# Attention keys on TensorE: 162 contracted rows as two runs of 81, or as 128 for all images and 64 on one half of the array for each pair

## The reference, cut to what matters

```python
q_flat = x.reshape(bs, 1, c * hw)
k_flat = k1.reshape(bs, 1, c * hw)
kq = jnp.stack([q_flat, k_flat], axis=2).reshape(bs, 2 * hw, c)
a = jax.nn.relu(_bn(jnp.einsum('oi,bic->boc', se_att_w1, kq), se_att_bn))
```

## Time and profile before

| | us |
|---|---|
| median of 3 runs | 1763.16 (1757.49 to 1765.74) |
| profiled execution, its time | 1758.98 |
| profiled execution, its span | 1757.3 |
| PE busy | 1375.9 |
| DVE busy | 1140.7 |
| ACT busy | 802.5 |
| POOL busy | 649.3 |

### The profile page before, as it was taken

How to read it: one execution, slowest core, us unless ns; L and a number is a source line. 1 busy time by engine, 2 the same in 40 slices (tenths; PEclk the granted TensorE clock), 3 DMA queues, 4 the chain that set the end, 5 groups by cost and what they waited for, 6 DMA issues and landing times.

```text
span 1757.3 us, 38235 instructions
## 1 busy us (share of the span) xinstructions
PE 1375.9 (78%) x9764; PEld 1122.8 (64%) x9765; DVE 1140.7 (65%) x3074; ACT 802.5 (46%) x1779; POOL 649.3 (37%) x561
## 2 busy tenths in 40 slices
PE   0297888889999999999755555499999999999300
PEld 0286888856666666666555555388888888888300
DVE  7795333328676767676488888566666666666493
ACT  0393444434443444443399998233333333333250
POOL 0161111113333333333066667245454545445200
PEclk9997787879999999999555555699999999999755
DMA  8535453566767675764133433423332323232475
GB/s 305 129 90 194 182 190 142 196 191 162 178 147 181 145 181 147 177 149 111 50 111 123 127 125 124 137 88 87 88 93 87 87 87 96 86 94 73 188 312 242
DMA packets 259238, 250.50 MB, mean 143 GB/s; under 512 B 150105, under 2 KB 234414, under 8 KB 255172
## 3 DMA queue, kind: packets, MB, share of 16 engines
q1 hardware_dynamic: 238895, 196.95, 38.5%
q0 software_dynamic: 20320, 53.28, 9.2%
HBM read 152.07 MB, written 105.57 MB: 147 GB/s over the span
## 4 chain that ended last, share of the span: by engine, by line
PE 68%; DVE 11%; ACT 7%; DMA 6%; issue 3%; SPq 3%; DVEq 0%; ACTq 0%; POOLq 0%; POOL 0%
PE ps L690 14%; PE ps L675 13%; PE ps L514 6%; PE ps L497 5%; PE ps L463 4%; PE ps L541 3%; PE ps L569 3%; PE ps L565 2%; DMA u_d<-in_zstrings 2%; ACT pool_ L1255 2%; PE ps L524 2%; PE ps L659 2%; DVE big L1211 2%; PE ps L533 2%; PE ps L567 2%
## 5 line engine op out<-in xcount | busy, mean ns | idle before, releaser
L1482 POOL DMA_INDIRECT y_d<-pool_,to_s x176 | 254.7, 1447 | 282.8 <-DVE pool_ L1171 248.2
L690 PE MATMUL ps<-pool_,aux 128*128 x2112 | 248.1, 273 | 5.1 <-DVE aux L1163 3.2
L675 PE MATMUL ps<-aux,pool_ 128*128 128x256 f16 x2112 | 246.2, 273 | 0.8 <-ACT aux L1383 0.6
L690 PEld LDWEIGHTS ps<-pool_,aux 128*128 128x128 f16 x2112 | 197.5, 98 | 50.0 <-issue 23.7
L675 PEld LDWEIGHTS ps<-aux,pool_ 128*128 x2112 | 206.3, 98 | 25.4 <-issue 1.5
L1383 ACT ACTIVATE aux<-ps,b_s 128x256 f32<-128x256 f32 x352 | 138.0, 474 | 161.9 <-DVE aux L1163 161.6
L1462 POOL DMA_INDIRECT rows_d<-aux,idx_s x162 | 160.0, 988 | 109.6 <-DVE idx_s L1074 60.2
L1171 DVE SCALAR_TENSOR_TENSOR pool_<-ps,pool_ 128x512 f32<-128x512 f32 x88 | 60.9, 692 | 138.9 <-PE ps L690 138.9
L1454 POOL DMA_DIRECT2D pool_<-v_d x64 | 50.0, 781 | 272.5 <-PE ps L571 271.1
L1375 ACT ACTIVATE aux<-ps 128x512 f16<-128x512 f32 x88 | 52.5, 597 | 173.7 <-PE ps L659 173.7
L514 PE MATMUL ps<-pool_,se_w_s 81*81 81x512 f32 x256 | 118.7, 607 | 5.4 <-DMA pool_<-k_d 5.4
(11 more groups left out here) (202 smaller groups left out, 3104.7 us busy)
## 6 DMA issues: line engine op xcount, KB each, us to landing
pool_<-rows_d SPq DMA_DIRECT2D x88, 258.0 KB
pool_<-y_d SPq DMA_DIRECT2D x18, 1152.0 KB, 8.6
big<-in_x SPq DMA_DIRECT2D x2, 5184.0 KB, 21.5
xn_d<-big SPq DMA_DIRECT2D x16, 648.0 KB, 3.0
v_d<-aux SPq DMA_DIRECT2D x64, 162.0 KB, 2.0
ks_d<-aux SPq DMA_DIRECT2D x64, 162.0 KB, 1.9
pool_<-xn_d SPq DMA_DIRECT2D x32, 324.0 KB
pool_<-k_d SPq DMA_DIRECT2D x32, 324.0 KB
```

Source lines behind the costliest of these rows:

```text
L675: last = nc.tensor.matmul(o, w_s[:, a, bass.ds(e * (4 * PIECE) + (k * HID + j * 128), 128)], xh_s[:, par, b, k * SLOTS:(k + 1) * SLOTS], s ...
L690: last = nc.tensor.matmul(ps[:, 6 + par, s * C:(s + 1) * C], hh_s[:, par, a, j, s * 128:(s + 1) * 128], w_s[:, b, bass.ds(e * (4 * PIECE) ...
L1482: nc.gpsimd.indirect_dma_start(out=y_d[:, :], out_offset=bass.IndirectOffsetOnAxis(ap=to_s[:, par, k:k + 1], axis=0), in_=yo_s[:, par, k, ...
```

## The change

Before, each pair of images takes two matmuls of 81 contracted rows (x, then k1), each with 512 moving columns. After, a first matmul contracts 128 rows (x rows 1 to 80 and k1 rows 0 to 47) for both pairs, and a second one 64 rows (x row 0, fifteen rows whose weights are zero, and k1 rows 33 to 80, of which the first fifteen have zero weights): for the pair n = 0 on partitions 0 to 63, for n = 1 on partitions 64 to 127. The number of matmuls stays at four a group, each 512 columns wide. The order changes: both 128-row matmuls, then both 64-row ones, and `se1_p` of n = 0 comes after the third instead of the second. The builder of instructions takes the part of the array from the operands' start partition and size: rows 0 to 63 or 64 to 127 for the last two.

The loads for `keys` become six a group in place of two, and move 128 x 4 + 2 x 64 x 2 = 768 rows of 1 KB in place of 648. Tiles behind `kq_s` move down by 4 KB in each partition. The weights are 128 x 2 x 81 with zeros where a row counts elsewhere.

```diff
-        se_w1_s = sb("se_w1_s", [HW, 2, HW])
+        se_w1_s = sb("se_w1_s", [128, 2, HW])
...
-        kq_s = take(HW, 2, 2, G, C)
+        kqa_s = take(128, 2, G, C)
+        kqb_s = take(128, 2, G // 2, C)
...
                     if not first:
                         sp.wait_ge(S["se1_p"], 2 * g - 2)
-                    for k, src in enumerate((xn_d, k1_d)):
-                        sp.dma_start(kq_s[:, par, k],
-                                     src[rows, :].rearrange("b (i j) -> i b j", j=C)).then_inc(S[f"kq_in{par}"], 16)
+                    xq, kq = (d[rows, :].rearrange("b (i j) -> i b j", j=C) for d in (xn_d, k1_d))
+                    for dst, src in ((kqa_s[0:80, par], xq[1:HW]), (kqa_s[80:128, par], kq[0:48])):
+                        sp.dma_start(dst, src).then_inc(S[f"kq_in{par}"], 16)
+                    for n in range(2):
+                        two = slice(2 * n, 2 * n + 2)
+                        for dst, src in ((kqb_s[64 * n:64 * n + 16, par], xq[0:16, two]),
+                                         (kqb_s[64 * n + 16:64 * n + 64, par], kq[HW - 48:HW, two])):
+                            sp.dma_start(dst, src).then_inc(S[f"kq_in{par}"], 16)
...
-                pe.wait_ge(S[f"kq_in{par}"], 32 * (i + 1))
+                pe.wait_ge(S[f"kq_in{par}"], 96 * (i + 1))
                 if not first:
                     pe.wait_ge(S["a_c"], 2 * g)
                 for n in range(2):
-                    for k in range(2):
-                        last = nc.tensor.matmul(ps[0:HW, n, :], se_w1_s[:, k, :],
-                                                kq_s[:, par, k, 2 * n:2 * n + 2, :].rearrange("p b j -> p (b j)"),
-                                                start=k == 0, stop=k == 1)
-                    last.then_inc(S["se1_p"], 1)
+                    nc.tensor.matmul(ps[0:HW, n, :], se_w1_s[:, 0, :],
+                                     kqa_s[:, par, 2 * n:2 * n + 2, :].rearrange("p b j -> p (b j)"),
+                                     start=True, stop=False)
+                for n in range(2):
+                    half = slice(64 * n, 64 * n + 64)
+                    nc.tensor.matmul(ps[0:HW, n, :], se_w1_s[half, 1, :],
+                                     kqb_s[half, par, :, :].rearrange("p b j -> p (b j)"),
+                                     start=False, stop=True).then_inc(S["se1_p"], 1)
...
+    wx, wk = i["conv_se_att_w1"].T.reshape(2, HW, HW)
+    se_w1 = np.zeros((128, 2, HW), f)
+    se_w1[0:80, 0], se_w1[80:128, 0] = wx[1:], wk[0:48]
+    for n in (0, 64):
+        se_w1[n, 1], se_w1[n + 31:n + 64, 1] = wx[0], wk[48:]
```

More of the change, by code:

```diff
@@ L1563 @@
         "key_bias": np.broadcast_to(i["conv_se_key_b"], (128, HW)),
-        "se_w1": i["conv_se_att_w1"].T.reshape(2, HW, HW).transpose(1, 0, 2), "se_bn": i["conv_se_att_bn"].T,
+        "se_w1": se_w1, "se_bn": i["conv_se_att_bn"].T,
         "se_w2": se_w2, "sa_w1": sa_w1, "sa_bn": halves(i["conv_sa_att_bn"].T), "sa_w2": sa_w2,
```

## The result

| | before | changed |
|---|---|---|
| median, us | 1763.64 (1757.49 to 1765.74, 4 runs) | 1745.18 (1739.83 to 1746.1, 4 runs) |
| profiled execution, its time | 1758.98 | 1739.83 |
| profiled execution, its span | 1757.3 | 1738.1 |

The ratio is 0.9895, with a 95% interval of 0.9873 to 0.9917: 18.5 us faster, clear of the 0.5% that the prediction named as the measurement's limit.

A forecast was written before the change was run, and what follows sets the result against it. PE was taken to bound the attention stage: 28 groups at 0.10 us plus 0.2 for the first gave 3.0, plus 0.7 at the start, 3.7 us saved. On the median's scale that meant 1759.5 us, range 1749 to 1773.

The forecast's parts named there:

- What bounds the stage: Attention stage, 440 to 813 us: PE is always busy at full clock, so PE time saved there is saved.
- the 0.91 us of slack ahead of `band`: DVE's last mask ends 0.91 us before `band` starts, so even 0.54 us saved in `keys` fits.
- The 128-row matmuls for free: In `keys`, columns streamed set the cost, so contracting 128 rows for 81 costs nothing; 0.43 us a record.
- The step that failed: 64-row matmuls in `keys`: records start in program order, so one of four half-array records is hidden, 0.43 us a group.
- rival 2: Cheap changes of shape (1750 us) or full overlap of all four half-array records in `keys` (1747 us); chance 0.20.
- The price of two changes: `keys` switches PE to half rows and back each group, costing 0.27 to 0.375 us.
- the reading by the gap: From gaps in `band`, plus weight loads no longer hidden: two changes of shape cost 0.375 us a group.
- the one by a sum over `band`: Eight `band` records take 1.25 us against 0.71 expected: 0.135 us for each of four changes, 0.27 for two.
- The rule cited against the change: For `keys`' changes to half rows: a change of tiling mode drains TensorE; the rule gives no drain's price.
- Loads: no cost: Six load issues for two take 1.6 us more, within 4.8 us of queue slack and 7 us of landing slack.
- A full spread over sixteen engines: Loads of 80, 48 and 16 partitions using all sixteen DMA engines would transfer in 2.3 us in place of 3.2.
- The stage's start: PE's wait for the first `keys` load shortens by 0.7 us, bounds -1.6 to +1.6.

The follow-up runs named there:

- same-half run: The changed kernel with both 64-row matmuls on the same half of the array (partitions 0 to 63), loads unchanged: 1772.52 us, ratio to before 1.0054.
- two-by-two run: The changed kernel with a further zero-weight 64-row matmul behind each 64-row matmul, on the same half: 1771.47 us, one execution.
- all-rows run: The changed kernel with the second matmuls contracting all 128 rows, zero weights on the other pair's half, loads unchanged: 1758.66 us, ratio to before 0.9977.

## Why the prediction was wrong

- **What bounds the stage: right.** What `keys` saved shows undiminished in the distance of groups, and the 0.91 us of slack ahead of `band` sufficed.
- **The 128-row matmuls for free: right.** Their four records hold PE 1.81 us, of which 0.09 is the change behind them.
- **The step that failed** is "If PE starts them in order, the second of n0 must wait for the first (same rows), the first of n1 may run beside the second of n0, and the second of n1 comes last: three times 0.43 in place of four. I take this, 0.43 us a group". It booked one record of overlap, and the overlap is two, 0.853 us a group (same-half run). The two-by-two run shows why: the halves do not keep a common order. That "every stretch of PE's timeline that I read shows records starting in program order" was no evidence. Overtaking can only be seen where two neighbours use different parts of the array, and the kernel before has no such neighbours in the loop: a matmul on all columns stands between any two narrow ones. The overlapping case stood in the prediction as part of rival 2 with its sum, 0.86 less the price of the changes, 1747 us; it was given too little of a chance, and the range ended above it.
- **The price of two changes** was given as 0.27 to 0.375, and 0.354 was measured. For rows the reading by the gap (0.375) came near, and the one by a sum over `band` (0.27) was too low. The sum was not wrong for columns: the reordered `band` gives 0.13 a change there too. What failed in it is that a price measured on columns was carried over to rows. The sum used the middle, 0.32 or 0.33, which is close to 0.354.
- **The rule cited against the change**, from the Trainium skill, TensorEngine Tiling (Array Packing), Key Properties (a change of mode drains, tiles operate independently), fits both numbers: 0.167 us for each of four changes, and independent halves. The Trainium skill, TensorE: Matmul & The Clock Gate, Part 3, has matmuls start and end in program order. For matmuls on different halves of the rows the two-by-two run contradicts it (eight records in 1.72 + 0.17 us), and the measurement decides. So does it for what the prediction drew from that page, an overlap of one record of four: it is two.
- **Loads: no cost, right, for a partly wrong reason.** The queue's six issues take 2.9 us and not 2.4 (starts 0.51 apart), and there is still time left. A full spread over sixteen engines was expected to bring a faster landing. The shares rose, as forecast, to 1.14 and 1.16 (rows below). The rate was 237 and then 169 GB/s, first above and then below the 205 of the earlier trace rows, and earlier loads may still be among the 237. From the first issue to the end of the transfers it took about as long as before: from 606.34 to about 611.7, and from 616.09 to about 621.4.
- **The stage's start** was given 0.7 us. From the first `keys` to the fifth it took 47.1 us for 48.4 before. The wait for the first load hardly changed: 4.86 us (row below) for 5.08. In the profiled executions of the seven kernels with six loads the first `keys` began at 376.7 to 378.8 us, for 379.05 and 379.11 in the two with two loads. So up to 2 us of such a difference is not the form of the loads, and what the form gives stays open.

```profile
376.83 3.70 PE L519 MATMUL ps<-pool_,se_w_s 128*81 128x512 f32 x4 [4.86 <-DMA pool_<-k_d]
```

The sum took 0.10 us for a group and it was 0.503. The difference times 28 is 11.3 us. That, and the 4.4 us gained outside the loop where the sum had 0.9, are the 14.8 us between the 3.7 forecast and the 18.5 measured.

DMA in the changed kernel. The loads for `keys` are issued from 606.34 to 608.90, behind eight others issued from 601.4 on; columns as in rows 2:

```profile
609.00:610.00 1.00, 1.00 (x8) 0.66 (x8) 0.96 (x2) 0.08 (x1) 0.00 (x0) 1.00 1.14 237
610.00:611.00 1.00, 1.00 (x8) 0.68 (x6) 0.77 (x2) 0.00 (x0) 0.00 (x0) 1.00 1.16 169
611.00:612.00 1.00, 1.00 (x9) 0.57 (x8) 0.56 (x1) 0.00 (x0) 0.00 (x0) 1.00 0.59 119
```

## What to carry to other kernels

Two fp32 matmuls of 64 rows on different halves of the array run fully at once here, also when another matmul waits ahead of them for the other half. But each change between half and full rows cost 0.167 to 0.177 us: count both, and keep matmuls of one shape together. Where TensorE never idles, such changes are worth looking for: reordering four matmuls of `band` by shape was worth 46 us, more than twice the change studied. Stop when another engine's slack is used up: with all wide ones first, the loop was slower.

## What the runs showed that was not expected

- A matmul on a free half of the rows overtook an earlier, not yet begun matmul on the other half: eight records of 0.43 us in 1.89 us.
- Narrow matmuls on different columns (96 to 127 and 0 to 31) overlap too, starting 0.01 us apart, where nothing wide stands between them; in the old order a wide one always did.
- A change of rows cost 0.167 us (four a group) to 0.177 (two a group), a change of columns in `band` an estimated 0.13.
- After waits of 2 to 3 us for a load early in the stage PE ran at the lower clock level, for about 3 us in the changed kernel and for about 12 in the same-half run; in the all-rows run, after a wait of 2.17 us, it did not.
